# Experts of two mixtures: rows transposed two tiles ahead with reordered stores, gate weights carried behind the rows, and accumulating transfers in place of the sums

## The chip, the cores and the metric

The kernel runs on one core of a Trainium2 chip. The metric is the device time of one execution in microseconds. The engines are PE (matrix products and transposes), DVE (vector), ACT (scalar activation), POOL (GpSimd, which also issues all indirect DMAs here) and SP (which issues the plain DMAs). Each runs its own instructions in order; they meet in semaphores.

## The reference

An image batch x (16, 128, 16, 16) goes through two convolution layers and then, as 4096 tokens of 128 channels, through four more layers, each added to its input:

```python
x = x + _L0_conv_ref(_gn(x), ...)
x = x + _L1_conv_ref(_gn(x))
t = _to_tokens(x)
t = t + _L2_attn_ref(_ln_t(t), ...)      # softmax attention
t = t + _L2_ffn_ref(_ln_t(t), ...)       # first mixture of experts, hidden 256
t = t + _L3_attn_ref(_ln_t(t), ...)      # linear attention
t = t + _L3_ffn_ref(_ln_t(t), ...)       # second mixture of experts, hidden 512
```

A mixture of experts takes, for every token, the 2 best of 8 experts by a router, and adds their outputs with softmax weights:

```python
topv, topi = jax.lax.top_k(gate_logits, K)
w = jax.nn.softmax(topv, axis=-1)
for e in range(n_experts):
    h = jax.nn.silu(jnp.einsum('bsd,df->bsf', x, W[e])) * jnp.einsum('bsd,df->bsf', x, V[e])
    y = y + gw[..., e:e + 1] * jnp.einsum('bsf,fd->bsd', h, W2[e])
```

## The kernel before

The tokens stand in on-chip memory as T, 128 partitions by 32 tiles by 128 channels. The stages run one after the other, with all engines meeting at the end of each: the convolutions, softmax attention, `route` and `experts` of the first mixture (names with `d_`), `linear_attention` (`e_`), `route`, `experts` and `combine` of the second mixture (`f_`).

**route** normalises the rows and stores them in memory (`xn_dram`, row p*32+t for partition p and tile t), computes the router's scores, picks two experts per token, and sorts the 8192 token and expert pairs into 71 tiles of 128 slots of one expert each. It leaves lists: which token stands in each slot (`gather`), where its result goes (`scatter`, second mixture only), the expert of each tile, the slot of each token (`slot`), and the two softmax weights per token (`weight`, lines 1735 to 1738), from `ratio` that ACT makes.

**experts** runs over the 71 tiles. For a tile n, POOL gathers 128 rows (line 1809, `xg`, 4 buffers), PE transposes them (1852), ACT copies the transposed rows rounded (`copy_x`, 1914, `x_high`), DVE takes the remainder (`low_x`, 1937, `x_low`), PE multiplies by the gate and up weights in three passes (`gate_up`, 1862 or 1865), ACT makes silu (1908), DVE the product (`hidden`, 1943), PE transposes that (1874), ACT copies it (1920), PE multiplies by the output weights (`down`, 1883), DVE copies the result out of the accumulator (`result`, 1949, `y`, 8 buffers). In the turn of tile n each engine's program has these in a fixed order: PE gate_up(n), transpose_x(n+1), transpose_h(n-1), down(n-2); ACT silu(n), copy_x(n+1), copy_h(n-1); DVE low_x(n+1), hidden(n), result(n-2). POOL gathers three tiles ahead, and a gather waits until the transpose has freed its buffer. The results of the first mixture are stored by SP in slot order (1800); those of the second are scattered by POOL, a row for each token and choice (1815), with the scatter of tile n-3 behind the gather of tile n+3.

Beside the first sixteen tiles of the first mixture, the gate and up weights of the second are read in sixteen pieces (`f_raw`, two buffers, line 1177, on SP, a piece ahead of each store), rounded by ACT (1181) and split by DVE (1190); a buffer is loaded again when DVE has split what was in it.

**linear_attention** begins with the sum of the first mixture: for each pair of tiles, POOL gathers the two result rows of each token into `e_yg` (1261, four gathers a pair), DVE multiplies each by its weight and adds it to T (1393, 64 operations), then the row moments follow (1118). At the end POOL adds the attention's output to T (1269). **combine** loads the scattered results of the second mixture (1981), scales the second choice on ACT (1993), adds the first with its weight on DVE (2009) and the second on POOL (2002), and stores the output in eight parts (1985).

## Time and profile before

| | us |
|---|---|
| times of three runs | 969.58, 969.69, 978.5 (median 969.69) |
| the profiled execution | 975.88 |
| its span in the trace | 974.1 |
| second experts, first gather to last scatter issued | 726.13 to 943.89 |
| linear attention, first gather to the next stage | 553.57 to 669.95 |
| mean granted TensorE clock | 0.871 of full speed |

Over the whole span PE is busy 746.4 us (77%), DVE 544.4 (56%), ACT 456.9 (47%) and POOL 437.2 (45%). These shares are averages over stages that have different limits, so the rows further down are taken from single stages. In a timeline, the bracket at the end of a row is the time in which the engine stood idle before the instruction, with what released it; "issue" means that it waited for nothing that the profile shows. SPq and POOLq are the issuing side of these engines. An indirect DMA has a duration on POOL, which is the time in which POOL writes it; its landing is counted from the start of the issue to the arrival of the data.

### The profile page before, as it was taken

Reading aid. Unit: us, or ns where it says so; the run is one execution under the profiler, and the core shown is the slowest. Engines: PE = TensorE matmul, PEld = TensorE weight load, DVE = VectorE, ACT = ScalarE, POOL = GpSimd, SP = SyncE. Lnnn points to the kernel's source line nnn. Section 1 sums busy time; section 2 is a strip of 40 time slices with the busy share of each in tenths; the row PEclk is TensorE's granted clock in tenths of the full one; section 3 lists DMA queues with packets and bytes.
Section 4 is the critical chain, followed back from the end, with each engine's and each line's share of the span. In section 5 each row is a group of like instructions: output and inputs, shape, how many; then the busy total and the mean of one; then the engine's idle time right before and its main releaser. Section 6 shows DMA issues by size and latency. Waiting matters only on the chain. (4 is left out here: it accounts for less than half of the span.)

```text
span 974.1 us, 17847 instructions
## 1 busy us (share of the span) xinstructions
PE 746.4 (77%) x4853; PEld 590.5 (61%) x4853; DVE 544.4 (56%) x1589; ACT 456.9 (47%) x1147; POOL 437.2 (45%) x464
## 2 busy tenths in 40 slices
PE   3797978989998736769999535566479999999960
PEld 1575846666665535446666424554367888888850
DVE  6587946777775559354444255776573333333326
ACT  1994435767775314444444334552144444444424
POOL 5000444655652060434444277831015666666734
PEclk9899887999997755899999867987559999999995
DMA  2000000000000240452222211102201111111107
GB/s 97 1 0 19 3 1 2 2 0 0 0 1 2 77 140 1 119 147 64 66 66 66 54 49 50 49 16 76 98 8 34 44 44 47 42 47 41 50 19 259
DMA packets 34197, 46.24 MB, mean 47 GB/s; under 512 B 8227, under 2 KB 22887, under 8 KB 33872
## 3 DMA queue, kind: packets, MB, share of 16 engines
q1 hardware_dynamic: 25264, 27.66, 8.8%
q0 software_dynamic: 8864, 17.72, 6.9%
q8 instruction: 36, 0.59, 0.3%
q14 instruction: 33, 0.27, 0.1%
HBM read 30.21 MB, written 15.60 MB: 47 GB/s over the span
## 5 line engine op out<-in xcount | busy, mean ns | idle before, releaser
L1809 POOL DMA_INDIRECT d_xg<-d_normed,d_gather x71 | 68.3, 961 | 104.5 <-PE ps L1852 79.6
L1047 DVE TENSOR_REDUCE negmax<-ps 128x2 f32<-128x512 f32 x128 | 82.6, 688 | 51.9 <-PE ps L881 51.1
L1809 POOL DMA_INDIRECT f_xg<-f_normed,f_gather x71 | 69.0, 971 | 78.5 <-SPq L1763 55.0
L1908 ACT ACTIVATE f_silu<-ps 128x512 f32<-128x512 f32 x71 | 42.5, 598 | 118.9 <-PE ps L1862 118.9
L1937 DVE TENSOR_TENSOR f_x_low<-ps,f_x_high 128x128 fp32r<-128x128 f32 x71 | 20.7, 292 | 135.5 <-ACT f_x_high L1914 135.5
L1815 POOL DMA_INDIRECT f_results<-f_y,f_scatter x71 | 71.9, 1013 | 54.4 <-issue 39.3
L788 ACT ACTIVATE prob<-ps 128x512 f32<-128x512 f32 x128 | 69.6, 598 | 44.4 <-PE ps L900 44.4
L1261 POOL DMA_INDIRECT e_yg<-d_results,d_slot_u x64 | 61.0, 953 | 32.9 <-issue 18.2
L1883 PE MATMUL ps<-f_w_out,f_hT 128*128 x568 | 75.2, 275 | 0.7 <-DVE f_y L1949 0.7
L1883 PEld LDWEIGHTS ps<-f_w_out,f_hT 128*128 128x128 f32 x568 | 69.0, 192 | 0.9 <-issue 0.9
L1937 DVE TENSOR_TENSOR d_x_low<-ps,d_x_high 128x128 fp32r<-128x128 f32 x71 | 20.6, 290 | 73.6 <-ACT d_x_high L1914 73.6
L1908 ACT ACTIVATE d_silu<-ps 128x256 f32<-128x256 f32 x71 | 27.1, 382 | 67.5 <-PE ps L1865 67.5
L725 POOL TENSOR_SCALAR q_low<-q,lower 128x512 fp32r<-128x512 f32 x16 | 24.9, 1559 | 66.3 <-ACT q L768 45.5
L1865 PE MATMUL ps<-d_w_high,d_x_high 128*128 x71 | 35.7, 503 | 23.9 <-DVE d_x_low L1937 15.8
L1862 PE MATMUL ps<-f_w_high,f_x_high 128*128 x142 | 51.7, 445 | 2.7 <-DVE f_x_low L1937 2.7
L898 PE MATMUL ps<-qa,ka 32*128 32x256 f32 x256 | 42.7, 348 | 11.8 <-DVE qb L1053 8.9
L1345 PE MATMUL ps<-ident,e_xn 128*128 128x128 f32 x32 | 9.0, 374 | 55.0 <-ACT e_xn L1311 55.0
L1943 DVE TENSOR_TENSOR f_h<-ps,f_silu 128x512 f32<-128x512 f32 x71 | 48.3, 681 | 1.8 <-ACT f_silu L1908 1.7
L1883 PE MATMUL ps<-d_w_out,d_hT 128*128 x284 | 48.2, 292 | 0.1
L327 PE MATMUL ps<-fcol,wimg 128*128 (+1 forms) x160 | 41.0, 404 | 5.9 <-ACT wimg L283 5.5
L1862 PE MATMUL ps<-f_w_high,f_x_low 128*128 x142 | 44.8, 396 | 0.0
L1862 PE MATMUL ps<-f_w_low,f_x_high 128*128 x142 | 44.6, 395 | 0.0
(353 smaller groups left out, 2105.0 us busy)
## 6 DMA issues: line engine op xcount, KB each, us to landing
d_results<-d_y SPq DMA_DIRECT2D x71, 64.0 KB
f_raw<-in_f_in SPq DMA_DIRECT2D x16, 256.0 KB, 2.8
f_ys<-f_results SPq DMA_DIRECT2D x8, 512.0 KB, 7.3
X<-in_x SPq DMA_DIRECT2D x4, 512.0 KB, 5.5
d_normed<-X SPq DMA_DIRECT2D x8, 256.0 KB, 2.0
d_raw<-in_d_in SPq DMA_DIRECT2D x8, 256.0 KB, 2.8
f_normed<-X SPq DMA_DIRECT2D x8, 256.0 KB, 2.0
f_w_out<-in_f_out SPq DMA_DIRECT2D x1, 2048.0 KB, 8.2
```

Source lines behind the costliest of these rows:

```text
L327: last = nc.tensor.matmul(ps[:, 2 + b, a * PIX:(a + 1) * PIX], wimg[:, a, t, :], rhs.rearrange("p n r c -> p (n r) c"), start=(t == 0), st ...
L788: nc.scalar.activation(prob[:, h].rearrange("p t q -> p (t q)"), ps[:, h % 2, :], ACT.Exp, scale=SCALE).then_inc(prob_ready, 1)
L898: nc.tensor.matmul(o, ka[rows, b, g, keys], qa[rows, b, g, :], start=True, stop=False)
L1047: nc.vector.tensor_reduce(negmax[:, :, h // HG, col:col + 1], ps[:, 2 + h % 2, :].rearrange("p (t k) -> p t k", t=2), AX_X, ALU.max, negat ...
L1261: nc.gpsimd.indirect_dma_start(yg[:, n % 4, t, c, :], None, first.y_dram, bass.IndirectOffsetOnAxis(ap=first.slot[:, c, tile:tile + 1], ax ...
L1809: nc.gpsimd.indirect_dma_start(xg[:, n % 4, :], None, moe.xn_dram, bass.IndirectOffsetOnAxis(ap=moe.gather[:, n:n + 1], axis=0)).then_inc( ...
L1815: nc.gpsimd.indirect_dma_start(moe.y_dram, bass.IndirectOffsetOnAxis(ap=moe.scatter[:, n:n + 1], axis=0), y[:, n % RING, :], None, bounds_ ...
L1862: ins = nc.tensor.matmul(o, x[:, n % 2, :], of_expert(w, n)[:, cols], start=(i == 0), stop=(i == len(passes) - 1))
L1883: ins = nc.tensor.matmul(Y(n), hT[:, n % 2, c * P:(c + 1) * P], moe.w_out[:, bass.ds(e, 1), c, :].rearrange("p e c -> p (e c)"), start=(c ...
L1908: nc.scalar.activation(silu[:, n % 2, :], GATE(n), ACT.Silu).then_inc(silu_ready, 1)
L1937: nc.vector.tensor_tensor(xT_low[:, n % 2, :], XT(n), xT[:, n % 2, :], ALU.subtract).then_inc(x_ready, 1)
L1943: nc.vector.tensor_tensor(h[:, n % 2, :], UP(n), silu[:, n % 2, :], ALU.mult).then_inc(h_ready, 1)
```

## The change

**Experts.** Rows are transposed two tiles ahead instead of one: the first two tiles' transpose, copy_x and low_x stand ahead of the loop, and in the turn of tile n PE has gate_up(n), transpose_x(n+2), ACT silu(n), copy_x(n+2), DVE hidden(n), low_x(n+2). POOL gathers four tiles ahead. SP's store of the first mixture comes three turns later in its program, and with it behind the loads of the weight pieces.

**Gate weights.** The weights are computed earlier in `route` as eight columns a token (`gates`, zero but for the two chosen experts) and stored behind the 128 channels of each row of `xn_dram`, which now has 136 columns and the order of the tokens (t p). A gathered row so brings its gates. A new DVE operation per tile, `slot_gates`, multiplies the eight columns by a one-hot of the tile's expert (`of_tile`, made in `route`) and sums them; it waits for the gather, and gather(n+4) now waits for slot_gates(n). `result` multiplies by that gate where it copied.

**Sums.** In linear attention, POOL's indirect DMAs add the rows straight into T (`compute_op=ALU.add`); the row of the second choice waits until that of the first has landed. The final addition to T goes from POOL to DVE. In the second mixture the output is filled with T at the head of `route`, and the scatters add into it; each waits until the one before has landed, since a token's two rows may stand in different tiles. `combine` is gone.

```diff
@@ route, SP
+            if out is not None:
+                sp.dma_start(out.rearrange("(t p) c -> p t c", p=P), T[:]).then_inc(tokens_stored, 16)
...
+            sp.wait_ge(gates_ready, 1)
+            sp.dma_start(rows_of[:, :, C:], gates[:]).then_inc(gates_stored, 16)
             sp.wait_ge(xn_stored, 16 * (TILES // GROUP))
+            sp.wait_ge(gates_stored, 16)
+            if out is not None:
+                sp.wait_ge(tokens_stored, 16)
@@ route, DVE
+            dve.wait_ge(ratio_ready, 1)
+            step(nc.vector.tensor_scalar(share[:, 0], ratio[:], 1.0, None, ALU.add))
+            step(nc.vector.reciprocal(share[:, 0], share[:, 0]))
+            step(nc.vector.tensor_tensor(share[:, 1], ratio[:], share[:, 0], ALU.mult))
+            step(nc.vector.tensor_tensor(gates[:], chosen[:, 0], by_tile(share[:, 0]), ALU.mult))
+            step(nc.vector.tensor_tensor(same[:], chosen[:, 1], by_tile(share[:, 1]), ALU.mult))
+            nc.vector.tensor_tensor(gates[:], gates[:], same[:], ALU.add).then_inc(gates_ready, 1)
...
+            nc.vector.tensor_scalar(moe.of_tile[:, :, 0:1], passed[:, :, 0:1], -1.0, 1.0, ALU.mult, ALU.add)
+            nc.vector.tensor_tensor(moe.of_tile[:, :, 1:], passed[:, :, 0:E - 1], passed[:, :, 1:], ALU.subtract)
@@ experts, SP
-                for n in range(TILES_IN):
+                for n in range(TILES_IN + 3):
                     if split is not None and n + 2 < split.pieces:
                         split.load(sp, n + 2)
-                    sp.wait_ge(y_ready, n + 1)
-                    sp.dma_start(moe.y_dram[n * P:(n + 1) * P, :], y[:, n % RING]).then_inc(stored[n % RING], 16)
+                    if n >= 3:
+                        store(n - 3)
@@ experts, POOL
                 if n >= 4:
                     pool.wait_ge(xT_ps, n - 3)
+                    pool.wait_ge(gate_ready, n - 3)
...
             def scatter(n):
                 pool.wait_ge(y_ready, n + 1)
+                if n > 0:
+                    pool.wait_ge(stored[(n - 1) % RING], 16 * ((n - 1) // RING + 1))
                 nc.gpsimd.indirect_dma_start(
-                    moe.y_dram, bass.IndirectOffsetOnAxis(ap=moe.scatter[:, n:n + 1], axis=0),
-                    y[:, n % RING, :], None, bounds_check=TOK * moe.TOP - 1,
-                    oob_is_err=False).then_inc(stored[n % RING], 16)
+                    out, bass.IndirectOffsetOnAxis(ap=moe.scatter[:, n:n + 1], axis=0),
+                    y[:, n % RING, :], None, bounds_check=TOK - 1, oob_is_err=False,
+                    compute_op=ALU.add).then_inc(stored[n % RING], 16)
@@ experts, DVE
+            def slot_gates(n):
+                dve.wait_ge(gathered[n % 4], 16 * (n // 4 + 1))
+                if n >= 4:
+                    dve.wait_ge(y_ready, n - 3)
+                if n > 0:
+                    dve.wait_ge(gate_ready, n)
+                nc.vector.tensor_tensor_reduce(product[:], xg[:, n % 4, C:], moe.of_tile[:, n, :], 1.0, 0.0,
+                                               ALU.mult, ALU.add, gate[:, n % 4:n % 4 + 1]).then_inc(gate_ready, 1)
@@ linear_attention, POOL
+            def add_rows(c, n):
+                if c == 1:
+                    pool.wait_ge(added[0][n % 4], 32 * (n // 4 + 1))
                 for t in range(2):
...
+                    nc.gpsimd.indirect_dma_start(
+                        T[:, tile, :], None, first.y_dram,
+                        bass.IndirectOffsetOnAxis(ap=first.slot[:, c, tile:tile + 1], axis=0),
+                        compute_op=ALU.add).then_inc(added[c][n % 4], 16)
...
+            for n in range(2, N + 1):
                 if n < N:
-                    gather(n)
-                if n >= 8:
-                    add_output(n - 8)
+                    add_rows(0, n)
+                add_rows(1, n - 1)
@@ linear_attention, DVE
             def moments(at, first_item, last):
-                dve.wait_ge(combined, at.n + 1)
+                dve.wait_ge(added[1][at.b4], 32 * (at.round + 1))
```

Three places in the order of the instructions. The first is SP at the head of the first experts: line 1177 (after: 1176) loads a weight piece, line 1800 (1799) stores a tile's result. Before:

```order
L1177 DMA f_raw<-in_f_in 128x512 x2
L1177 DMA f_raw<-in_f_in 128x512 [waits f_w_low_rd]
L1800 DMA d_results<-d_y 128x128 [waits d_y_rd]
L1177 DMA f_raw<-in_f_in 128x512 [waits f_w_low_rd]
L1800 DMA d_results<-d_y 128x128 [waits d_y_rd]
```

and after:

```order
L1176 DMA f_raw<-in_f_in 128x512 x2
L1176 DMA f_raw<-in_f_in 128x512 [waits f_w_low_rd] x4
L1799 DMA d_results<-d_y 128x128 [waits d_y_rd]
L1176 DMA f_raw<-in_f_in 128x512 [waits f_w_low_rd]
L1799 DMA d_results<-d_y 128x128 [waits d_y_rd]
```

The store between two loads is now that of three tiles before, so that its `d_y` is older. The second place is DVE in a tile of the first experts, well into the loop. Before:

```order
L1937 TENSOR_TENSOR d_x_low<-ps,d_x_high 128x128 [waits d_x_high_rd]
L1943 TENSOR_TENSOR d_h<-ps,d_silu 128x256 [waits d_h_ps,d_silu_rd]
L1949 COPY d_y<-ps 128x128 [waits d_stored3,d_y_ps]
L1937 TENSOR_TENSOR d_x_low<-ps,d_x_high 128x128 [waits d_x_high_rd]
L1943 TENSOR_TENSOR d_h<-ps,d_silu 128x256 [waits d_h_ps,d_silu_rd]
```

and after:

```order
L1965 TENSOR_TENSOR d_h<-ps,d_silu 128x256 [waits d_h_ps,d_silu_rd]
L1949 TENSOR_TENSOR d_x_low<-ps,d_x_high 128x128 [waits d_x_high_rd]
L1958 ISA d_product,d_gate<-d_xg,d_of_tile 128x8 [waits d_gate_rd,d_y_rd,d_gathered2]
L1958 ISA d_gate 128x1
L1972 TENSOR_SCALAR d_y<-ps,d_gate 128x128 [waits d_gate_rd,d_stored0,d_y_ps]
L1965 TENSOR_TENSOR d_h<-ps,d_silu 128x256 [waits d_h_ps,d_silu_rd]
```

low_x stands behind hidden and is that of two tiles later; slot_gates is two instructions, behind low_x and ahead of the result. The third place is POOL in the second experts, from the first scatter on (the names of the semaphores are those of earlier holders of the same number). Before:

```order
L1809 DMA f_xg<-f_normed,f_gather 128x128 x4
L1809 DMA f_xg<-f_normed,f_gather 128x128 [waits c_ln_chain] x3
L1815 DMA f_results<-f_y,f_scatter 8192x128 [waits c_headsT_rd]
L1809 DMA f_xg<-f_normed,f_gather 128x128 [waits c_ln_chain]
L1815 DMA f_results<-f_y,f_scatter 8192x128 [waits c_headsT_rd]
```

and after:

```order
L1815 DMA f_xg<-f_normed,f_gather 128x136 x4
L1815 DMA f_xg<-f_normed,f_gather 128x136 [waits c_kl_rd,c_headsT_rd] x4
L1824 DMA out_tokens<-f_y,f_scatter 4096x128 [waits c_kb_rd]
L1815 DMA f_xg<-f_normed,f_gather 128x136 [waits c_kl_rd,c_headsT_rd]
L1824 DMA out_tokens<-f_y,f_scatter 4096x128 [waits c_tok_rd,c_kb_rd]
L1815 DMA f_xg<-f_normed,f_gather 128x136 [waits c_kl_rd,c_headsT_rd]
L1824 DMA out_tokens<-f_y,f_scatter 4096x128 [waits c_bo_added,c_kb_rd]
```

Every gather has a second wait (for the gate), and every scatter but the first a second one (for the landing of the scatter before); one more gather stands ahead of the first scatter.

## Rows read from the trace of the kernel before

**Rows 1.** Table by stage, second experts: busy us of PE, PEld, DVE, ACT, POOL; clock; DMA.
```profile
726.00:946.00 220.00, 213.37 (x1355) 187.48 (x1354) 77.57 (x213) 90.59 (x214) 140.86 (x142) 0.99 0.15 42
```

**Rows 2.** Timeline, one tile of the first experts: start, duration, engine, line, out<-in, idle before.
```profile
470.26 0.50 PE L1865 MATMUL ps<-d_w_high,d_x_high 128*128 x1 [0.20 <-issue]
...
471.06 0.27 PE L1852 MATMUL ps<-ident,d_xg 128*128 128x128 f32 x1
...
471.26 0.38 ACT L1908 ACTIVATE d_silu<-ps 128x256 f32<-128x256 f32 x1 [1.19 <-PE ps L1865]
...
471.39 0.68 PE L1883 MATMUL ps<-d_w_out,d_hT 128*128 x4
471.55 0.27 ACT L1914 ACTIVATE d_x_high<-ps 128x128 fp32r<-128x128 f32 x1
471.61 0.94 POOL L1809 DMA_INDIRECT d_xg<-d_normed,d_gather  x1 [1.08 <-PE ps L1852]
...
471.85 0.29 DVE L1937 TENSOR_TENSOR d_x_low<-ps,d_x_high 128x128 fp32r<-128x128 f32 x1 [1.20 <-ACT d_x_high L1914]
472.06 0.41 DVE L1943 TENSOR_TENSOR d_h<-ps,d_silu 128x256 f32<-128x256 f32 x1
...
472.28 0.49 PE L1865 MATMUL ps<-d_w_high,d_x_high 128*128 x1 [0.21 <-issue]
```

**Rows 3.** Timeline, conversion of the second layer's weight pieces (ACT first, last; DVE).
```profile
396.94 0.63 ACT L1181 ACTIVATE f_w_high<-f_raw 128x512 fp32r<-128x512 f32 x1
...
409.04 0.69 DVE L1190 TENSOR_TENSOR f_w_low<-f_raw,f_w_high 128x512 fp32r<-128x512 f32 x1 [0.85 <-ACT f_w_high L1181]
...
438.33 0.63 ACT L1181 ACTIVATE f_w_high<-f_raw 128x512 fp32r<-128x512 f32 x1 [0.82 <-DMA f_raw<-in_f_in]
```

**Rows 4.** Timeline of SP: a store and a load in the first experts, combine's loads.
```profile
410.49 0.33 SPq L1800 DMA_DIRECT2D d_results<-d_y  x1
410.86 0.43 SPq L1177 DMA_DIRECT2D f_raw<-in_f_in  x1
...
950.23 4.16 SPq L1981 DMA_DIRECT2D f_ys<-f_results  x8
```

**Rows 5.** Timeline of POOL in linear attention, and the next stage's first operation.
```profile
553.57 0.94 POOL L1261 DMA_INDIRECT e_yg<-d_results,d_slot_u  x1 [14.44 <-POOLq L1763]
...
639.08 0.94 POOL L1261 DMA_INDIRECT e_yg<-d_results,d_slot_u  x1 [0.30 <-issue]
...
669.97 0.24 POOL L1549 IOTA f_up_to<- 128x128 f32 x1 [5.57 <-POOLq L1204]
```

**Rows 6.** Timeline of POOL in the second experts: first gather, first scatters, last scatter.
```profile
726.13 0.97 POOL L1809 DMA_INDIRECT f_xg<-f_normed,f_gather  x1 [54.98 <-SPq L1763]
...
741.09 1.02 POOL L1815 DMA_INDIRECT f_results<-f_y,f_scatter  x1 [4.36 <-DVE f_y L1949]
...
744.00 1.01 POOL L1815 DMA_INDIRECT f_results<-f_y,f_scatter  x1 [0.60 <-issue]
...
943.89 0.98 POOL L1815 DMA_INDIRECT f_results<-f_y,f_scatter  x1 [0.84 <-DVE f_y L1949]
```

**Rows 7.** DMA issues (out<-in, engine, count, KB each, median us to landing).
```profile
f_raw<-in_f_in SPq DMA_DIRECT2D x16, 256.0 KB, 2.8
...
out_tokens<-T SPq DMA_DIRECT2D x8, 256.0 KB, 3.4
...
f_xg<-f_normed,f_gather POOLq DMA_INDIRECT x71, 2.6
...
f_results<-f_y,f_scatter POOLq DMA_INDIRECT x71, 2.3
...
e_yg<-d_results,d_slot_u POOLq DMA_INDIRECT x64, 2.5
```

**Rows 8.** Timeline of DVE in the second route: its wait for PE.
```profile
697.79 0.42 DVE L1681 COPY f_total<-ps 128x256 f32<-128x256 f32 x1 [2.13 <-PE ps L1633]
```

**Rows 9.** Timeline of DVE in linear attention: moments of the last pair.
```profile
648.78 0.49 DVE L1118 BATCH_NORM_STATS2 ln_stats<-T 128x6 f32<-128x128 f32 x2
```

More of the change, by code:

```diff
@@ L1746, in _, with experts @@
             nc.vector.tensor_scalar(empty[:], token[:], 0.0, NEVER, ALU.is_equal, ALU.mult)
-            step(nc.vector.tensor_scalar(target[:], token[:], 2.0, -2.0, ALU.mult, ALU.add))
-            step(nc.vector.tensor_tensor(target[:], target[:], empty[:], ALU.add))
-            nc.vector.scalar_tensor_tensor(moe.scatter[:], found[:, 1], 0.0, target[:], ALU.is_gt, ALU.add)
-def experts(nc, top, moe, split=None):
+            step(nc.vector.tensor_scalar(target[:], token[:], 1.0, None, ALU.subtract))
+            nc.vector.tensor_tensor(moe.scatter[:], target[:], empty[:], ALU.add)
+def experts(nc, top, moe, split=None, out=None):
     ps, ident = top.ps, top.ident
@@ L1766, in experts @@
         sem = lambda *names: [k.sem(f"{tag}_{s}") for s in names]
[L1767 removed]
+        xg = sb("xg", [P, 4, C + moe.E])
+        product = sb("product", [P, moe.E])
+        gate = sb("gate", [P, 4])
         xT = sb("x_high", [P, 2, P], F32R)
@@ L1888, in _ @@
             load_expert(0)
-            transpose_x(0)
+            for n in range(2):
+                transpose_x(n)
             for n in range(TILES_IN + 2):
@@ L1920, in copy_h @@
                 nc.scalar.activation(hT[:, n % 2, :], HT(n), ACT.Copy).then_inc(hT_ready, 1)
-            copy_x(0)
+            for n in range(2):
+                copy_x(n)
             for n in range(TILES_IN + 1):
@@ L1948, in result @@
                     dve.wait_ge(stored[n % RING], 16 * (n // RING))
-                nc.vector.tensor_copy(y[:, n % RING, :], Y(n)).then_inc(y_ready, 1)
-            low_x(0)
+                dve.wait_ge(gate_ready, n + 1)
+                nc.vector.tensor_scalar(y[:, n % RING, :], Y(n), gate[:, n % 4:n % 4 + 1], None,
+                                        ALU.mult).then_inc(y_ready, 1)
+            for n in range(2):
+                low_x(n)
             for n in range(TILES_IN + 2):
-                if n + 1 < TILES_IN:
-                    low_x(n + 1)
                 if n < TILES_IN:
                     hidden(n)
+                if n + 2 < TILES_IN:
+                    low_x(n + 2)
+                if n < TILES_IN:
+                    slot_gates(n)
                 if n >= 2:
@@ L2129, in program @@
             second.allocate_lists(Kit(nc, layer))
-            route(nc, top, second, d["f_router"], d["f_out"])
-            experts(nc, top, second)
-            combine(nc, top, second, out)
+            route(nc, top, second, d["f_router"], d["f_out"], out=out)
+            experts(nc, top, second, out=out)
 def kernel(**inputs):
```

143 lines of the change are left out of this document (40 added, 103 removed).

## Prediction

> **What bounds the kernel now.** I read the table by stage first, then a timeline of one repeating piece of each stage that the change touches, then the DMA landings. In the second mixture of experts PE is busy 213.37 of 220 us [rows 1]: it is the bound there, and whatever the change takes off other engines in that stretch gives nothing. The first mixture is a ring of waits. The first gate/up matmuls of neighbouring tiles start 2.02 us apart (470.26, 472.28), and between them lie silu (471.26), copy_x (471.55), low_x (471.85) and a start of PE; PE's other work lies inside [rows 2]. Its first sixteen tiles are slower: ACT converts the sixteen pieces of the second layer's weights from 396.94 to 438.33, 2.76 us apart, and waits for their transfer, as in the row of 438.33 [rows 3]. SP issues each load right behind a store (410.49, then 410.86), so it is held by the store's wait for y [rows 4]. In linear attention POOL is the clock: an indirect DMA takes 0.94 and 0.30 passes before the next, about 1.25 each, 64 of them and 16 additions from 553.57 on; it starts the next stage only at 669.97, 5.57 after its last operation [rows 5]. Behind the experts comes combine: the last scatter is issued at 943.89 [rows 6] and lands 2.3 later [rows 7], the loads of combine start at 950.23 [rows 4], the span ends at 974.1.
>
> **Step A, rows transposed two tiles ahead.** The operations are the same ones, earlier, and the ring copy_x, low_x, gate_up closes over two tiles. In the fifteen gaps of the first sixteen tiles the load no longer stands behind a late store; what is left is the ring of two raw buffers: landing 2.8 [rows 7], ACT's 0.63 and DVE's 0.69 [rows 3], three hand-overs of 0.05 at most: 4.25 for two pieces, 2.13 each. 15 x (2.76 - 2.13) = 9.4 gained. For the other 54 gaps I look for the next ring. gather(n+4) now waits for slot_gates(n), which DVE reaches only behind low_x(n+2), and that needs the gather of n+2. One turn serves two tiles: landing 2.6 [rows 7], PE's transpose 0.27 with about 0.1 to ACT, copy_x to low_x 0.30, low_x 0.21 until DVE takes the next operation, slot_gates (two operations on 8 columns) 0.16 by estimate from that, POOL's start 0.28 behind the end of what it waits for (471.33 to 471.61) [rows 2]: 3.9, so 1.95 a tile against 2.02, and 54 x 0.07 = 3.8. Bounds: nothing if the ring is 0.14 longer; 54 x 0.37 = 20 if it had slack, as PE's own work is 1.13 up to the down product (470.26 to 471.39) and 0.5 to 0.68 for that [rows 2]. I take 3.8, since each term of the ring has a row near it, less 0.4 for the second transpose ahead of the first product: **-12.8**.
>
> **Step B, gates behind the rows.** Six DVE operations come into each route, three of them of 128x256 like f_total's (0.42) and three of 128x32, some 2 together; they stand where DVE now waits 2.13 for PE [rows 8]. Two operations come, three go, later in the route. I take +0.4 each, **+0.8**; without the wait as cover it is +2 each. The store of the gates has 4096 pieces of 32 B. Its bound is the 3.4 that a store of 512 pieces takes [rows 7] eight times, 27 us; it is issued while DVE still has everything from f_total (697.79) on to do [rows 8], which lasts 28 us, until the first gather at 726.13 [rows 6]. The stores of the rows now have pieces of 512 B and may take that 3.4 too, with the whole route to land in. Multiplying y by its gate takes the place of a copy of the same size, and in the second experts slot_gates has room, with DVE busy 77.57 of 220 [rows 1]: nothing.
>
> **Step C, linear attention.** The 64 sums on DVE and the 16 additions on POOL go; the 64 gathers become accumulating DMAs into T. From the first issue (553.57) to the last (639.08) pass 85.5 us now [rows 5], of which 63 gaps of 1.25 are 78.8; of the other 6.7 the additions go, and I leave 2 for POOL's small operations. So the last is issued at 634.4 and landed at 636.9, and moments of the last pair, which runs at 648.78 now [rows 9] and only waits for that, comes 11.9 earlier. The second row of a token waits for the first, which is issued five issues ahead (6.2 us), so that wait is covered up to a landing of 6.2. On DVE 64 operations go and 16 come. At the end 5.57 pass between POOL's last operation and the next stage [rows 5]; POOL's last work would now lie 30 us back, so DVE's end sets the next stage, about 1 behind it: 4.5 more. **-16.4**. The price of an accumulating issue is not in the trace. Below it is bounded by the plain one, 0.94; above by half again as much, 1.41, if each row needs a second source beside the source and target it has, and then this step is 30 worse, +13.
>
> **Step D, accumulating into the output.** combine goes: without it the span would end some 4 us behind the last landing, as the loads at 950.23 [rows 4] come 4.0 behind 946.2: 950.2. 950.2 - 974.1 = **-23.9**. The price stands on POOL. Each scatter waits until the one before has landed. Behind that wait it needs 0.8 until it is issued, as 943.89 stands 0.8 behind the end of the last y [rows 6]. So a scatter takes L + 0.83, L being its landing, against the 2.91 between two scatters now (741.09, 744.00; the second waits for nothing, so that is POOL's own turn too) [rows 6]. Behind the waiting scatter stands gather(n+4), and PE then waits for that. The first scatter comes a tile later than 741.09, at 744: gather(7) stands ahead of it and waits for slot_gates(3), which DVE reaches in the turn after result(0). The last landing is 744 + 70 x (L + 0.83) + L, and 946.2 before. L is not in the trace. Its lower end is the plain scatter, 2.3: +19. Its upper end is a gather and then a scatter with one issue shared, 2.6 + 2.3 - 1.0 = 3.9: +133. The nearest row is the plain gather from memory in linear attention, 2.5 [rows 7], since the add must read HBM too, and the two reads go together: P = 3.33, **+33**. Filling the output with T is 2 MB at the head of the route, eight times the 3.4 of [rows 7] at most, with over 50 us to land (669.97 to 726.13) [rows 5, 6]. PE would be idle 0.4 of a tile; its granted clock is 0.99 now [rows 1], and should it fall, that 0.4 is the cover.
>
> POOL's row says that an indirect transfer of 64 KB lands in 2.3 to 2.6 whichever way it goes [rows 7]. The Trainium skill ("DMA: Bandwidth & Descriptors", Anatomy of one DMA) gives 2.0 us fixed and bytes / 436 GB/s; with the target read as well that is 2.30 in place of 2.15, an estimate of +0.15 on the scatter's row, L = 2.45 and a sum 4 lower. The same page's rules for kernel authors say that an accumulating DMA reads its target and writes it later with nothing held in between, which is why the wait can't be dropped; no row here shows that.
>
> **Sum.** -12.8 + 0.8 - 16.4 + 33 - 23.9 = -19.3. It is made on the profiled execution, 975.88 (span 974.1), which lies 6.2 above the median of 969.69; the difference is applied to the median: **950**.
>
> **Rivals.**
> 1. *The accumulating scatter lands later* (the other side). Place: POOL's wait for stored ahead of every scatter of the second experts. Price: 71 us for each us of L. For it: memory is read and then written. Against: gather and scatter rows differ by only 0.3. L = 2.77 makes the change worth nothing; 2.91 makes it slower by 1%; at 3.2 the time is 950 + 50 = 1000, at 3.9 it is 1050.
> 2. *The accumulating issue is dearer on POOL.* At 1.41, linear attention loses 30 and, as landing counts from the issue, the scatters 71 x 0.47 = 33: 1013. For it: POOL's 0.94 is work on 128 rows, and a second source is more of it. Against: nothing measured. The Trainium skill ("Collectives: The Full Stack", Why ReduceScatter is half of AllGather) says that an add needs two source reads, with two descriptors a chunk; by that this rival would hold, and no row here shows it.
> 3. *The landing is as short as the plain scatter's, or hidden.* L = 2.3 gives 936; at 2.08 or below POOL's own turn of 2.91 rules, the term is +4, and the time is 921.
> 4. *Two tiles ahead does something else than I cost.* If the ring through slot_gates has slack, 16 more are gained (934); if it is 0.1 longer, the 3.8 go (954). For the first: a gather takes POOL only 0.94 of a tile's 2.02 [rows 2]. Against: the gather waits for the gate by the order of DVE.
>
> **How the numbers follow.** About 1% (9.7 us) is what a measurement of this kernel can tell from no change. Forecast, L from 2.36 to 2.63, 940 to 960: 0.37. Rival 3, or the good half of 4, 921 to 940: 0.14. L of 2.63 to 2.91, or mishaps of that size, 960 to 979: 0.17. Beyond 979: 0.32, of it rival 1 with 0.18 and rival 2 with 0.14. So faster 0.51, same 0.17, slower 0.32. Below 930 (L under 2.2) I leave 0.06, above 1000 (L over 3.2, or rival 2) 0.14: range 930 to 1000. The likeliest case's own range is 940 to 960.
>
> **What would show it.** In the profile after: first experts, f_w_high 2.1 apart over sixteen tiles and gate/up 1.95 apart behind them, with gather waiting for d_gate; linear attention, accumulating issues 1.25 apart, the last by 635, moments of the last pair near 637, next stage under 1 us behind DVE; second experts, scatters 3.33 apart and PE idle 0.4 a tile for the gather; landing of the scatters 2.5; end 4 us behind the last landing. The prediction is wrong if L leaves 2.36 to 2.63, if an issue takes over 1.0, or if POOL's gather isn't what the first experts wait for.

## The result, and the profile after

The changed kernel takes 1080.15 us (median; 1076.93 to 1087.09) against 969.63 before, a ratio of 1.1125 (95% interval 1.1042 to 1.1209): slower by 11%, where 950 with a range of 930 to 1000 was forecast. The profiled execution took 1079.49, its span is 1077.7, 103.6 more than before. By stages, from the first indirect DMA or plain DMA of each in the two timelines:

| stretch | before | after | change | forecast |
|---|---|---|---|---|
| all ahead of the first gather of the first experts | 390.1 | 386.9 | -3.2 | +0.4 |
| first experts, to the first transfer of linear attention | 163.5 | 179.2 | +15.7 | -12.8 |
| linear attention, to the load of the second router | 116.4 | 139.7 | +23.3 | -16.4 |
| second route, to the first gather | 56.2 | 51.9 | -4.3 | +0.4 |
| second experts, first gather to last scatter issued | 217.8 | 314.4 | +96.6 | +33 |
| the end | 30.2 | 5.7 | -24.5 | -23.7 |

The forecasts of the last two rows are the 33 and the -23.9 of the prediction, divided at the issue of the last scatter. Only the end came as forecast. The stretch ahead of the first gather ended between 380.9 and 390.6 in the profiled executions of all the kernels here, so its -3.2 says nothing of the change.

The groups of instructions that cost most, from the page of the changed kernel (line, engine, operation, out<-in, count; busy us, mean ns of one; idle before, with what ended most of it):

```profile
L1824 POOL DMA_INDIRECT out_tokens<-f_y,f_scatter x71 | 112.6, 1586 | 104.2 <-DMA out_tokens<-f_y,f_scatter 84.8
...
L1815 POOL DMA_INDIRECT d_xg<-d_normed,d_gather x71 | 70.7, 996 | 122.8 <-DVE d_gate L1958 92.3
...
L1258 POOL DMA_INDIRECT T<-d_results,d_slot_u x64 | 99.3, 1552 | 30.7 <-issue 18.8
```

An accumulating transfer now occupies POOL 1552 to 1586 ns, where the plain ones of [rows 5, 6] take 0.94 to 1.02 us. POOL waits 84.8 us for the scatters' own landing and 92.3 us for the gate ahead of the first experts' gathers. The landings, from the list of DMA issues:

```profile
f_raw<-in_f_in SPq DMA_DIRECT2D x16, 256.0 KB, 2.8
...
d_xg<-d_normed,d_gather POOLq DMA_INDIRECT x71, 2.5
f_xg<-f_normed,f_gather POOLq DMA_INDIRECT x71, 2.5
out_tokens<-f_y,f_scatter POOLq DMA_INDIRECT x71, 3.3
...
T<-d_results,d_slot_u POOLq DMA_INDIRECT x64, 3.2
```

The plain gathers land in 2.5, within 0.1 of before [rows 7]; the accumulating scatter needs 3.3 in place of 2.3, the accumulating gather 3.2 in place of 2.5, both counted from the start of their issue. So POOL in the second experts (timeline):

```profile
784.35 1.59 POOL L1824 DMA_INDIRECT out_tokens<-f_y,f_scatter  x1 [1.36 <-DMA out_tokens<-f_y,f_scatter]
786.25 0.99 POOL L1815 DMA_INDIRECT f_xg<-f_normed,f_gather  x1 [0.30 <-issue]
...
1067.71 1.55 POOL L1824 DMA_INDIRECT out_tokens<-f_y,f_scatter  x1 [1.98 <-DMA out_tokens<-f_y,f_scatter]
1072.03 1.55 POOL L1824 DMA_INDIRECT out_tokens<-f_y,f_scatter  x1 [2.76 <-issue]
```

Scatters stand 4.23 apart from the first (775.88) to the last (1072.03), 70 gaps in 296.15 us, against the 2.9 of [rows 6]. PE follows: of the 313 us from 757 to 1070 it is busy 225.68, where it was busy 213.37 of 220 [rows 1]:

```profile
757.00:1070.00 313.00, 225.68 (x1355) 181.97 (x1355) 98.09 (x355) 103.36 (x214) 180.73 (x141) 0.95 0.22 30
```

In linear attention POOL does little but issue, and the issues are 1.85 apart (timeline), against 1.25 [rows 5]:

```profile
601.05 1.54 POOL L1258 DMA_INDIRECT T<-d_results,d_slot_u  x1 [0.30 <-issue]
602.90 1.54 POOL L1258 DMA_INDIRECT T<-d_results,d_slot_u  x1 [0.30 <-issue]
```

In the first experts, a piece of the timeline with the hand-over that matters. `d_gate` is written by the second of slot_gates' two instructions, and the gather waits for it:

```profile
470.83 0.94 POOL L1815 DMA_INDIRECT d_xg<-d_normed,d_gather  x1 [0.95 <-DVE d_gate L1958]
...
472.17 0.29 DVE L1949 TENSOR_TENSOR d_x_low<-ps,d_x_high 128x128 fp32r<-128x128 f32 x1 [0.53 <-ACT d_x_high L1925]
...
472.46 0.08 DVE L1958 DVE_READ_ACCUMULATOR2_ANT d_gate<- 128x1 f32 x1
...
473.29 0.94 POOL L1815 DMA_INDIRECT d_xg<-d_normed,d_gather  x1 [1.52 <-DVE d_gate L1958]
```

The gate is done at 472.54, the gather begins at 473.29: 0.75 later, not the 0.28 of [rows 2]. The other 45 gathers that wait for the gate from 440 us on start 0.74 to 0.76 behind it. Gathers come in pairs 4.33 us apart (460.32, 464.61, 468.94, 473.29 in the timeline of POOL), 2.17 a tile, against 2.02 before. Over all 54 gaps behind the first sixteen tiles the mean is 2.31, because some gathers land late. The landings of line 1815, first from 395 to 436 us, beside the loads of the weight pieces, then from 440 to 553:

```profile
DMA to landing us min/median/max: 2.8/3.4/3.6
...
DMA to landing us min/median/max: 2.4/2.5/4.4
```

### The profile page after: what moved, and what is told of

It reads as the page before. It is cut to its first block and busy times, and to the rows that moved or that the text cites. A ratio compares the mean times of both kernels' runs of the same rounds, so it can differ in the third digit from the quotient of the medians.

```text
span 1077.7 us, 18335 instructions
## 1 busy us (share of the span) xinstructions
PE 752.8 (70%) x4853; PEld 580.9 (54%) x4853; DVE 562.4 (52%) x1802; ACT 467.1 (43%) x1115; POOL 498.0 (46%) x440
## 5 line engine op out<-in xcount | busy, mean ns | idle before, releaser
L1824 POOL DMA_INDIRECT out_tokens<-f_y,f_scatter x71 | 112.6, 1586 | 104.2 <-DMA out_tokens<-f_y,f_scatter 84.8
L1815 POOL DMA_INDIRECT d_xg<-d_normed,d_gather x71 | 70.7, 996 | 122.8 <-DVE d_gate L1958 92.3
L1258 POOL DMA_INDIRECT T<-d_results,d_slot_u x64 | 99.3, 1552 | 30.7 <-issue 18.8
L1892 PE MATMUL ps<-f_w_out,f_hT 128*128 x568 | 78.5, 283 | 0.6 <-DVE f_y L1972 0.6
L1861 PE MATMUL ps<-ident,f_xg 128*128 128x128 f32 x71 | 22.7, 319 | 72.3 <-DMA f_xg<-f_normed,f_gather 71.2
L1118 DVE BATCH_NORM_STATS2 ln_stats<-T 128x6 f32<-128x128 f32 (+1 forms) x128 | 31.0, 284 | 75.9 <-DMA T<-d_results,d_slot_u 56.0
L1861 PEld LDWEIGHTS ps<-ident,f_xg 128*128 128x128 f32 x71 | 9.8, 139 | 99.3 <-DMA f_xg<-f_normed,f_gather 98.0
L1861 PE MATMUL ps<-ident,d_xg 128*128 128x128 f32 x71 | 23.2, 330 | 44.9 <-DMA d_xg<-d_normed,d_gather 44.3
L1965 DVE TENSOR_TENSOR d_h<-ps,d_silu 128x256 f32<-128x256 f32 x71 | 30.1, 424 | 43.2 <-ACT d_silu L1919 43.2
L1861 PEld LDWEIGHTS ps<-ident,d_xg 128*128 128x128 f32 x71 | 10.3, 145 | 73.1 <-DMA d_xg<-d_normed,d_gather 71.9
L1925 ACT ACTIVATE f_x_high<-ps 128x128 fp32r<-128x128 f32 x71 | 19.6, 276 | 64.9 <-PE ps L1861 64.9
```

The costliest lines, as they stand in the source:

```text
L1118: last = nc.vector.bn_stats(top.ln_stats[:, bass.ds(t, 1), :].rearrange("p a s -> p (a s)"), top.T[:, bass.ds(t, 1), :].rearrange("p a c - ...
L1258: nc.gpsimd.indirect_dma_start(T[:, tile, :], None, first.y_dram, bass.IndirectOffsetOnAxis(ap=first.slot[:, c, tile:tile + 1], axis=0), c ...
L1815: nc.gpsimd.indirect_dma_start(xg[:, n % 4, :], None, moe.xn_dram, bass.IndirectOffsetOnAxis(ap=moe.gather[:, n:n + 1], axis=0)).then_inc( ...
L1824: nc.gpsimd.indirect_dma_start(out, bass.IndirectOffsetOnAxis(ap=moe.scatter[:, n:n + 1], axis=0), y[:, n % RING, :], None, bounds_check=T ...
L1861: nc.tensor.transpose(XT(n), xg[:, n % 4, 0:C], ident[:]).then_inc(xT_ps, 1)
L1892: ins = nc.tensor.matmul(Y(n), hT[:, n % 2, c * P:(c + 1) * P], moe.w_out[:, bass.ds(e, 1), c, :].rearrange("p e c -> p (e c)"), start=(c ...
```

## The experiments

All times are medians; each ratio is to the kernel before on the same chip. The kernel before had medians of 968.9 to 971.9 in these runs. The kernels down to half_rows change one thing in the changed kernel each; half_rows ran once. a_alone and a_add_dve start from the kernel before, b_kept from the changed one. On the chip of the four kernels from plain_scatter to a_add_dve the kernel before itself spread from 960.07 to 978.55, so differences of 1% between them are not resolved.

| kernel | us | ratio to before (95%) |
|---|---|---|
| the changed kernel | 1080.15 | 1.1125 (1.1042 to 1.1209) |
| gates_first | 1059.22 | 1.0863 (1.0767 to 1.0959) |
| one_wait | 1063.48 | 1.0957 (1.0891 to 1.1023) |
| plain_e | 1053.84 | 1.0834 (1.0784 to 1.0884) |
| two_tables | 999.91 | 1.0280 (1.0210 to 1.0350) |
| plain_scatter | 1008.23 | 1.0440 (1.0351 to 1.0529) |
| half_rows | 1066.39 | one run |
| a_alone | 930.23 | no interval; 917.69 to 934.0 |
| a_add_dve | 908.52 | 0.9418 (0.9324 to 0.9513) |
| b_kept | 922.80 | 0.9500 (0.9413 to 0.9587) |

The theory after this result: three prices make the change slow, and each is its own. An accumulating transfer occupies POOL 0.6 us longer, whatever waits for it (linear attention); its landing stands in a chain (second experts); and the gate ring is longer than costed (first experts). The rivals are named in the expectations.

### gates_first: the gate a turn earlier

```diff
                 if n < TILES_IN:
+                    slot_gates(n)
                     hidden(n)
                 if n + 2 < TILES_IN:
                     low_x(n + 2)
-                if n < TILES_IN:
-                    slot_gates(n)
```

> The changed kernel with one line moved: DVE computes slot_gates(n) ahead of hidden(n) instead of behind low_x(n+2). Theory: the first experts are held by the ring gather, transpose, copy_x, low_x, slot_gates, gather of 4.33 us per two tiles (2.17 a tile); with the gate a turn earlier that ring closes over three tiles and PE's own work (about 1.7 a tile) is the bound: gate/up 1.7 apart in the steady tiles, 2.1 to 2.4 in the first sixteen, first experts 25 to 35 us shorter, total 1045 to 1055. Rival: the place of slot_gates does not matter, the gather's landing and its hand-over are the ring wherever the gate stands: gate/up stay 2.1 to 2.2 apart, total 1075 to 1085.

1059.22, and the first experts took 145.2 us (389.9 to 535.1) in place of 179.2: 34 less, the gain of the theory. The total is above its range, the profiled execution (1056.2) by 1 us; its second experts took 318.0 against 314.4. Gate/up now start 1.47 to 1.9 apart in most of the steady tiles, with eight gaps of 2.2 to 2.9 among the 54, some 1.8 on the mean. So the place of slot_gates was what held the ring. The closest ones show that PE itself can do 1.5, less than the theory had for it:

```profile
468.12 0.48 PE L1874 MATMUL ps<-d_w_high,d_x_high 128*128 x1
...
469.65 0.47 PE L1874 MATMUL ps<-d_w_high,d_x_high 128*128 x1
...
471.13 0.47 PE L1874 MATMUL ps<-d_w_high,d_x_high 128*128 x1
```

These are the first matmuls of gate/up of three tiles in PE's timeline.

### one_wait: the gather with a single wait

```diff
                 if n >= 4:
-                    pool.wait_ge(xT_ps, n - 3)
                     pool.wait_ge(gate_ready, n - 3)
```

> The changed kernel with the gather's wait for the transpose left out; it is implied by the wait for the gate, which stays. Theory: the hand-over from the gate to the gather takes 0.75 us because the gather carries two waits, of which one is an instruction of its own; with one wait it takes about 0.28 as before, the ring of the first experts falls from 4.33 to 3.9 per two tiles, 16 us less, total about 1064. Rival: the hand-over from DVE to an indirect DMA on POOL takes 0.75 whatever the count of waits: total 1075 to 1085, hand-over unchanged.

1063.48, 16.7 less, as the theory said to within a microsecond; the first experts took 162.0 (381.4 to 543.4), 17.2 less. The hand-over in its timeline:

```profile
471.90 0.08 DVE L1957 DVE_READ_ACCUMULATOR2_ANT d_gate<- 128x1 f32 x1
...
472.25 0.95 POOL L1814 DMA_INDIRECT d_xg<-d_normed,d_gather  x1 [1.17 <-DVE d_gate L1957]
```

The gate is done at 471.98 and the gather starts at 472.25: 0.27, against 0.75 with two waits (0.26 to 0.28 in all 43 such gathers from 440 us on). So the 0.48 are a price of the second wait, not of the way from DVE to POOL; the pairs of gathers come 4.0 apart instead of 4.33.

### plain_e: linear attention without accumulation

```diff
-                        T[:, tile, :], None, first.y_dram,
-                        bass.IndirectOffsetOnAxis(ap=first.slot[:, c, tile:tile + 1], axis=0),
-                        compute_op=ALU.add).then_inc(added[c][n % 4], 16)
+                            yg[:, n % 4, t, c, :], None, first.y_dram,
+                            bass.IndirectOffsetOnAxis(ap=first.slot[:, c, tile:tile + 1],
+                                                      axis=0)).then_inc(gathered[n % 4], 16)
...
+                    nc.vector.tensor_tensor(t, t, yg[:, at.b4, :, c, :], ALU.add).then_inc((first_added, combined)[c], 1)
```

> The changed kernel with linear attention's accumulating transfers undone: plain gathers into a buffer, 32 additions of 128x256 on DVE (the rows come already weighted), the final addition still on DVE. Theory: what lengthened linear attention is the issue of an accumulating transfer on POOL, 1.55 against 0.94; plain gathers come 1.25 apart, the stage takes about 100 us against 140 in the changed kernel and 116 before, total 1038 to 1045. Rival: the longer landing (3.2) and the waits of the second row made it longer, or DVE becomes the bound with the additions: the stage takes 115 us or more, total 1055 or more.

The stage took 101.1 us (570.8 to 671.9) against 139.7, so the theory's 100; the total fell by 26 only, to 1053.84, 9 above the theory's range. Of the missing 12 us two stretches show most: its second route took 56.3 in place of 51.9 and its second experts 320.2 in place of 314.4, both of which the edit does not touch. The stage itself is settled: with plain gathers 1.25 apart and 32 additions on DVE it is also 15 us shorter than before.

```profile
602.62 0.94 POOL L1261 DMA_INDIRECT e_yg<-d_results,d_slot_u  x1 [0.30 <-issue]
603.87 0.94 POOL L1261 DMA_INDIRECT e_yg<-d_results,d_slot_u  x1 [0.30 <-issue]
```

(POOL's timeline: two gathers that wait for nothing, 1.25 apart.)

### two_tables: the chain without its link

```diff
-                if n > 0:
-                    pool.wait_ge(stored[(n - 1) % RING], 16 * ((n - 1) // RING + 1))
+                if n > 1:
+                    pool.wait_ge(stored[(n - 2) % RING], 16 * ((n - 2) // RING + 1))
                 nc.gpsimd.indirect_dma_start(
-                    out, bass.IndirectOffsetOnAxis(ap=moe.scatter[:, n:n + 1], axis=0),
+                    (out, moe.out_odd)[n % 2], bass.IndirectOffsetOnAxis(ap=moe.scatter[:, n:n + 1], axis=0),
```

> The changed kernel with the scatters of the second experts alternating between the output and a second table, each filled with the tokens, so that a scatter waits for the landing of the one two before it; the two tables are not summed. Theory: the wait for the landing is the bound of the second experts (3.3 landing and 0.9 until the next issue); without it POOL's own turn rules, 1.59 + 0.30 + 0.98 + 0.3 to 0.6, so 3.2 to 3.5 a tile against 4.23: 50 to 70 us less, total 1010 to 1030. Rival: the transfers themselves are slow (reading and writing back contend in memory) and scatters still come 4.0 or more apart: total 1060 or more.

999.91, 80 less than the changed kernel and 10 under the theory's range. From first to last the scatters stand 3.10 apart (776.3 to 993.1), 1.13 less; while gathers run between them it is 3.19, and POOL goes from one transfer to the next with 0.30 between them (timeline):

```profile
843.32 1.59 POOL L1826 DMA_INDIRECT f_out_odd<-f_y,f_scatter  x1 [0.30 <-DVE f_gate L1960]
845.22 0.99 POOL L1817 DMA_INDIRECT f_xg<-f_normed,f_gather  x1 [0.30 <-DMA out_tokens<-f_y,f_scatter]
846.51 1.59 POOL L1826 DMA_INDIRECT out_tokens<-f_y,f_scatter  x1 [0.30 <-DVE f_gate L1960]
```

1.59 + 0.30 + 0.99 + 0.30 = 3.18: this is POOL's own turn with an accumulating scatter. So the link to the landing before costs 70 x 1.13 = 79 us of the 97. Of the other 17, 14 are the longer turn (3.10 against the 2.90 between all scatters before) and 3 are the first scatter, which comes 18.2 behind the first gather in place of 15.0. The transfers as such, two in flight, don't hold anything up.

### plain_scatter: the wait without the addition

```diff
                 nc.gpsimd.indirect_dma_start(
                     out, bass.IndirectOffsetOnAxis(ap=moe.scatter[:, n:n + 1], axis=0),
-                    y[:, n % RING, :], None, bounds_check=TOK - 1, oob_is_err=False,
-                    compute_op=ALU.add).then_inc(stored[n % RING], 16)
+                    y[:, n % RING, :], None, bounds_check=TOK - 1,
+                    oob_is_err=False).then_inc(stored[n % RING], 16)
```

> The changed kernel with the addition left out of the second experts' scatters: each still waits until the one before has landed, but it writes its rows over those in the output. Theory: of the 1.3 us by which a tile of the second experts grew, the addition makes most, since it lengthens both the issue (1.59 against 1.01) and with it the landing (3.3 against 2.3), which stands in the chain; without it a scatter lands in 2.3, the chain takes 2.3 + 0.9 = 3.1 to 3.2 a tile and the total is 1000 to 1010. Rival: the wait itself costs that much whatever is transferred, and scatters stay 3.8 or more apart: total 1050 or more.

1008.23, in the theory's range; scatters 770.5 to 998.2, 3.25 apart. They take 1.01 to issue (timeline of POOL):

```profile
841.94 1.01 POOL L1824 DMA_INDIRECT out_tokens<-f_y,f_scatter  x1 [0.88 <-DVE f_y L1972]
843.26 0.97 POOL L1815 DMA_INDIRECT f_xg<-f_normed,f_gather  x1 [0.30 <-PE ps L1861]
845.09 1.01 POOL L1824 DMA_INDIRECT out_tokens<-f_y,f_scatter  x1 [0.85 <-DVE f_y L1972]
```

and land in 2.3, from the instructions of the scatter's line:

```profile
DMA to landing us min/median/max: 2.1/2.3/4.1
```

So the same chain with a plain transfer is 2.3 + 0.95 = 3.25, and the addition adds 0.98 to each turn, as much as its landing is longer (3.3 against 2.3). The formula of the prediction, landing plus a hand-over of 0.83, fits with 0.93 to 0.95 in its place. These are means; the usual turn is 3.17 here and 4.15 in the changed kernel, 0.85 to 0.87 over the landing, and a few late turns (4.6 to 5.5 in the changed kernel, seven of 70) make the rest. The 70 x 0.98 = 69 us here and the 79 of two_tables don't add up, since either edit shortens the same link. The rows above put most of POOL's waits on f_y and not on the landing: with the short landing the two come at nearly the same time, as y is late in its turn when the gathers are.

### half_rows: is the issue's price one of rows?

```diff
-                        T[:, tile, :], None, first.y_dram,
-                        bass.IndirectOffsetOnAxis(ap=first.slot[:, c, tile:tile + 1], axis=0),
+                        T[0:64, tile, :], None, first.y_dram,
+                        bass.IndirectOffsetOnAxis(ap=first.slot[0:64, c, tile:tile + 1], axis=0),
```

> The changed kernel with linear attention's accumulating transfers on 64 of 128 rows each, the other rows left out. Theory: the issue's price is one of rows, as the accumulating transfers leave one packet a row (144 packets each in the trace against 32 of a plain gather), so that (1.54 - 0.94)/(144 - 32) = 0.0054 us a packet and 72 packets take about 1.15, landing 2.7 to 2.9, issues 1.45 apart. Rival: the addition makes the issue dearer as an operation, whatever its rows: 1.45 or more, issues 1.75 or more apart.

1.41 (timeline below), so 0.13 less for half of the rows; the issues come 1.72 apart and land in 3.0. The theory of rows, with 1.15, falls, and the rival holds, if a little under its figures of 1.45 and 1.75.

```profile
602.77 1.41 POOL L1258 DMA_INDIRECT T<-d_results,d_slot_u  x1 [0.30 <-issue]
604.49 1.41 POOL L1258 DMA_INDIRECT T<-d_results,d_slot_u  x1 [0.30 <-issue]
```

The packets of the software queue in that stage, from the list of DMA queues (queue; packets, MB, share), with the kernel before:

```profile
q0 software_dynamic: 2048, 4.20, 17.8%
```

with the changed kernel:

```profile
q0 software_dynamic: 9216, 4.20, 26.1%
```

and with half_rows:

```profile
q0 software_dynamic: 5120, 2.10, 16.0%
```

For 64 transfers each: 32 packets a plain gather, 144 an accumulating one, 80 with half the rows. The sizes of all packets in the same windows, before and after:

```profile
DMA packets 2341, 4.44 MB, mean 48 GB/s; under 512 B 1056, under 2 KB 1312, under 8 KB 2336
...
DMA packets 9508, 4.44 MB, mean 33 GB/s; under 512 B 1056, under 2 KB 9504, under 8 KB 9504
```

Before, 1024 packets lie between 2 and 8 KB, 16 a gather, so eight rows are one packet of 4 KB; after there are none, and one row is one packet. The other 16 of a transfer are small, with or without the addition. 64 packets less save 0.13 us of issue; if the price is linear in packets, all 112 more of them would cost 0.23 of the 0.60. The rest, about 0.4, is then of the accumulating operation itself. That is an argument, as no plain transfer of half the rows was run; what POOL does in it no row shows.

### a_alone and a_add_dve: the first part by itself

On the kernel before, the transposes two ahead, the stores and AHEAD = 4 of the change, nothing else; and, in a_add_dve, the last addition of linear attention moved:

```diff
-                if n >= 8:
-                    add_output(n - 8)
...
+            def add_tokens(at, first_item, last):
+                dve.wait_ge(heads_ready, at.n + 3)
+                t = T[:, bass.ds(2 * at.n, 2), :]
+                nc.vector.tensor_tensor(t, t, heads[:, at.b], ALU.add).then_inc(tok_ready, 1)
```

> The kernel before with the first part alone: rows transposed two tiles ahead, first two ahead of the loop, stores three turns later, gathers four ahead; weights, sums, scatters and combine as before. Theory: without the wait for the gate the two tiles ahead free the ring of the first experts and PE is the bound, 1.6 to 1.7 a tile, 2.1 to 2.4 in the first sixteen: 20 to 30 us less than before, total 940 to 950. Rival: gather, transpose and copy are the ring whether or not a gate stands in it, gate/up stay 1.95 or more apart and the total is 960 or more.

> The same, and the final addition of linear attention on DVE instead of POOL, as the changed kernel has it. Theory: POOL is the clock of linear attention with its 64 plain gathers; without the 16 additions they come 1.25 apart throughout, the last one about 5 us earlier, and DVE's end alone sets the next stage: 12 to 17 us less than with the first part alone, total 925 to 935. Rival: DVE takes up what POOL sheds and the stage is as long as before: total as with the first part alone.

930.23, better than the theory's range. The first experts took 125.6 us (390.1 to 515.8) in place of 163.5, the steady tiles 1.49 apart (first matmuls of gate/up in PE's timeline), and the weight pieces 2.15 apart: sixteen from 396.6 to 428.9 (both below; the second is the line of ACT's conversion, with count, ns of one, first and last start).

```profile
447.82 0.48 PE L1870 MATMUL ps<-d_w_high,d_x_high 128*128 x1
...
449.30 0.48 PE L1870 MATMUL ps<-d_w_high,d_x_high 128*128 x1
...
450.77 0.48 PE L1870 MATMUL ps<-d_w_high,d_x_high 128*128 x1
```

The conversion of the pieces:

```profile
L1181 ACT ACTIVATE f_w_high<-f_raw x16: 630/632/642, 396.6 to 428.9; 128x512 fp32r<-128x512 f32 x16
```

The second experts gained too, 208.7 in place of 217.8, 2.80 a tile. PE is busy 205.90 us of the 210.80 from 688.3 to 899.1, much the same share as in [rows 1], so the busy share did not show that this was to be had.

With the addition on DVE the time is 908.52, the best of all here, 0.9418 of before: linear attention takes 104.6 (511.5 to 616.1) in place of the 116.3 of a_alone, 11.7 less, a little under the theory's lower end. The total is under the theory's 925 to 935. The profiled executions differ by 20.5 (928.97 and 908.46); of the rest, 4.4 lie in the second route (51.8 against 56.2, the same instructions, at another clock) and 5.3 ahead of the first experts, where the edit changes nothing.

### b_kept: the gates without accumulation

The changed kernel with slot_gates ahead of hidden, the gather's one wait, plain_e's linear attention, the kernel before's scatters, and a combine that only adds:

```diff
+                tiles = slice(i * STEP, (i + 1) * STEP)
+                nc.vector.tensor_tensor(T[:, tiles], T[:, tiles], ys[:, tiles, 0], ALU.add).then_inc(first_added, 1)
```

> The changed kernel with the gate weights kept behind the rows and everything that accumulates undone: slot_gates ahead of hidden, the gather waiting for the gate alone, plain gathers and 32 additions in linear attention, plain scatters of both rows of a token without the wait, and a combine that only adds (no scaling on ACT). Theory: the loss of the changed kernel lies in the accumulating transfers and in the ring through slot_gates, and the gates themselves cost 2 to 3 us in the routes and give back 2 to 5 in combine; the first experts take 1.5 to 1.6 a tile, the second 2.8 to 2.9, linear attention about 101, total 900 to 912, as much as the kernel with two tiles ahead and the addition on DVE (908.5). Rival: carrying the gates costs by itself, since slot_gates keeps the gathers late: first experts 1.7 or more a tile, total 920 or more.

922.80: 14 over a_add_dve, on the rival's side of the line between the two. Most steady tiles come 1.5 apart as there, but eight of the 54 gaps are 2.3 to 2.8, and the pieces of the first sixteen stand 2.38 apart (392.4 to 428.1), with DVE's subtraction of a piece ahead of the next gate. So the first experts took 140.1 against 126.7: carrying the gate costs 13 there even at the better place. Linear attention (101.2 against 104.6) and the end (26.7 against 29.9) gained a little over 3 each, and the second route took 59.8 against 51.8. Of these 8, 7.6 are PE's: its router products end 23.0 into the stage in place of 15.4, at a granted clock of 0.53 from 635.4 to 646.4, where a_add_dve has 0.86 from 625.1 to 636.1.

## Why the prediction was wrong, point by point

- **D, the landing.** The step that failed first: L was put at 2.5, by the nearest row, the plain gather, and it measured 3.3. The chain's formula was right (first scatter 18.2 behind the first gather, forecast 17.9; hand-over 0.93 on the mean, 0.85 in the usual turn, for 0.83). With L = 3.3 it gives 744 + 70 x 4.13 + 3.3 - 946.2 = +90 in place of 33; measured, and counted from the first gather, the last landing is 98 later. That alone is half of the miss, some 64 us of the 123 by which the profiled span lies over 974.1 - 19.3. Rival 1 had it, with a chance of 0.18 for L over 2.91. L is counted from the start of the issue. From its end the scatter's landing is 1.29 plain and 1.71 accumulating (2.3 - 1.01, 3.3 - 1.59), the gather's 1.56 and 1.66 (2.5 - 0.94, 3.2 - 1.54). So 0.58 of the 1.0 that L lies over the plain scatter are the longer issue, if nothing of the transfer goes on beside it; what makes the other 0.42 no row shows. A reading beside it was wrong as well: 2.91 is not POOL's own turn, which rival 3 took as its floor. In the kernel before POOL can do 2.60, where it catches up behind a late turn (timeline):

```profile
901.65 1.02 POOL L1815 DMA_INDIRECT f_results<-f_y,f_scatter  x1 [0.30 <-issue]
902.98 0.98 POOL L1809 DMA_INDIRECT f_xg<-f_normed,f_gather  x1 [0.30 <-PE ps L1852]
904.26 1.02 POOL L1815 DMA_INDIRECT f_results<-f_y,f_scatter  x1 [0.30 <-issue]
```

- **C and rival 2, the issue.** Forecast at 0.94 with 1.41 as an upper bound; measured 1.54 (1.59 for the scatter), above the bound. The bound came from a second source for each row; as far as half_rows tells, the rows are not the main price. Linear attention went to +23.3 where -16.4 was forecast and +13 was the bound. The rest of the step held: moments of the last pair wait for POOL alone, and DVE's end sets the next stage (the last statistics of rows end at 705.48, the router's load is issued at 705.75). Rivals 1 and 2 were taken as alternatives; both came, and then the sum lies above the range's end of 1000. The rule from the Trainium skill that was weighed as rival 2, two source reads for an add ("Collectives: The Full Stack", Why ReduceScatter is half of AllGather), pointed the right way; that they are two descriptors a chunk, no row here shows. The estimate from the Trainium skill's fit ("DMA: Bandwidth & Descriptors", Anatomy of one DMA) with both operands counted was 2.30, against the 3.3 of the trace, and the trace decides.
- **A, the ring through the gate.** Named and placed rightly, and in the steady tiles mis-sized by one term: 0.28 for POOL's start, from a gather with one wait, where two waits take 0.75. The other terms are 2.55 for the landing, 0.37 to copy_x, 0.31 to low_x, 0.21 and 0.16: 4.35 with the 0.75, and 4.33 was measured. So 2.17 a tile in place of 1.95, slower than the 2.02 of before; that is 12 of the 28 us of this step's miss. Late gathers, which no term of the ring holds (up to 4.4 for the usual 2.5), bring the mean to 2.31, 8 more. In the first sixteen tiles the load ring did come free (ACT no longer waits for the pieces), but the same gate ring kept the pieces 2.70 apart, not 2.13, and that is the other 8: there the gathers landed in 3.4 in place of 2.5, which in the sum of the ring is 0.9 of the 1.07 by which two tiles take longer than 4.33. The prediction let the load ring alone rule there, and took the same 2.6 for the gathers of all tiles. a_alone, without that ring, has 2.15. (The terms of the load ring add up to 4.27, not 4.25, which changes nothing.)
- **The slack bound.** 1.13 and 0.5 to 0.68 for PE's own work, 1.63 to 1.81 a tile, was too high: a_alone runs 1.49 a tile. And "whatever the change takes off other engines in that stretch gives nothing", of the second experts, was too strong: a_alone gained 9 there.
- **D, combine.** -23.9 forecast, -24.5 measured.
- **B.** The second route's DVE stretch from f_best to f_total grew by 0.38 (697.79 - 690.11 before, 729.57 - 721.51 after), as costed; the first by 3.25 (359.27 - 348.69, 357.14 - 343.31), over the 2 named for the case without cover. Operations of 128x256 took up to 1.40 there in place of 0.42, of the added ones and, with 1.37, already of those before; POOL was splitting weights beside them, and whether that is the cause was not tried.

The experiments show the sign of every part: transposes two ahead, the stores and the addition on DVE are worth some -60 by themselves. Counted from a_add_dve on, in the profiled executions, the gates behind the rows take 13 of that away in the first experts where they stand better, and 39 more as the change places them, with two waits on the gather. The accumulating transfers cost more than all of that, 35 in linear attention and 105 in the second experts, and give 24 back at the end.

## What to carry to other kernels

An operation that the trace does not show needs a bound from the dearest thing that it could be, and the range must hold the case that two such unknowns are dear at once. Before a plain transfer becomes an accumulating one, count what its landing will stand in: here it cost its issue outside a chain, and inside one its whole landing, each time. A new consumer in a ring of buffers belongs at the earliest place in its engine's program, and a wait that another already implies is better left out.

## What the runs showed of the hardware

- An accumulating indirect transfer of 128 rows of 512 B occupies POOL 1.54 to 1.59 us against 0.94 to 1.01, lands in 3.2 to 3.3 against 2.3 to 2.5, and leaves 144 packets (one a row) against 32 (one for eight rows), 16 small ones among them in both.
- A gather of the first experts with two waits starts 0.75 us after the one that comes last, with one wait 0.27. It is not so for every indirect DMA: the scatter of the kernel before, with a single wait, starts 0.78 behind the y that it waits for (943.11 to 943.89 in the timeline).
- The second route took 51.9 us after and 56.2 before, though it has more to do; gates_first, with the changed kernel's instructions there, took 56.2, and one_wait 51.7, so it is not the change's. PE's matmuls for the router are the bound there, and the granted clock differs (table by stage; the column ahead of the last two is the clock): 1.00, the 2.4 GHz level, through the stretch after, and 0.65 before, where the same products took nearly twice as long from about 681 on (eight of them 1.71 in place of 0.96). PE was busy in both stretches. It had stood idle 7.77 us ahead of the stage in the kernel before and 3.85 in the changed one, but that does not decide it: gates_first and one_wait have the same 3.85. What does stays open.

Before:

```profile
678.00:688.00 10.00, 10.00 (x64) 10.00 (x64) 3.15 (x13) 4.14 (x11) 0.00 (x0) 0.65 0.79 297
```

And after:

```profile
713.00:721.00 8.00, 7.97 (x74) 7.88 (x74) 3.92 (x16) 4.67 (x12) 0.00 (x0) 1.00 1.06 281
```
